# Scan of a state-space layer: u times D made by ScalarE in place and added as turns, in place of products with diagonals of D

## The reference, cut to what matters

```python
delta = softplus(dt_raw @ dt_proj_w.T + dt_proj_b)            # per token, 256 inner channels
A = -exp(A_log)
dA = exp(einsum('bti,is->btis', delta, A))                    # 16 states s
dBu = einsum('bti,bts->btis', delta * u, B_ssm)
h_t = dA_t * h_(t-1) + dBu_t                                  # the scan over 512 tokens
y_t = einsum('bis,bs->bi', h_t, C_t)
y = ys + u * D_param                                          # D_param: one number per inner channel
y = y * silu(z)
return y @ out_proj_w.T + residual
```

## Time and profile before

| | us |
|---|---|
| median of 3 runs | 1143.78 |
| the profiled execution's own time | 1146.79 |
| its span | 1144.8 |
| PE busy | 1031.4 (90%) |
| PEld busy | 797.5 (70%) |
| DVE busy | 896.6 (78%) |
| ACT busy | 822.5 (72%) |
| POOL busy | 516.9 (45%) |
| scans at L1084, x128 | 289.8 |
| idle of DVE before them | 31.7 |

### The profile page before, as it was taken

The page is one execution under the profiler, slowest core; times in us unless marked ns, Lnnn a source line. Parts: engine busy times, 40 slices in busy tenths (PEclk is TensorE's granted clock), DMA queues, the critical chain, the costliest instruction groups (busy, mean ns, idle before and its releaser), DMA issues. The chain is left out here.

```text
span 1144.8 us, 23452 instructions
## 1 busy us (share of the span) xinstructions
PE 1031.4 (90%) x7794; PEld 797.5 (70%) x7794; DVE 896.6 (78%) x1946; ACT 822.5 (72%) x1736; POOL 516.9 (45%) x322
## 2 busy tenths in 40 slices
PE   3876699999999999988997999999999999986997
PEld 3442589899899889858994555555555555555997
DVE  7698898889889888964764687878878787885565
ACT  4898898898988988735654676766767676761664
POOL 0288898898999988833550000110101010111354
PEclk9998699999999999999998999999999999998999
DMA  3000255555686676423332000000000000002331
GB/s 99 3 4 26 78 153 135 141 146 150 186 243 175 174 215 174 120 80 97 98 90 74 1 1 1 20 15 6 20 1 20 1 20 1 20 20 67 106 94 52
DMA packets 107782, 89.50 MB, mean 78 GB/s; under 512 B 35815, under 2 KB 85740, under 8 KB 107664
## 3 DMA queue, kind: packets, MB, share of 16 engines
q1 hardware_dynamic: 98784, 66.02, 22.1%
q0 software_dynamic: 5568, 12.66, 3.1%
q10 hardware_dynamic: 3312, 9.33, 2.7%
HBM read 71.49 MB, written 17.39 MB: 78 GB/s over the span
## 5 line engine op out<-in xcount | busy, mean ns | idle before, releaser
L1084 DVE TENSOR_TENSOR_SCAN h<-d_a,p_dbu 128x1024 f32<-128x1024 f32 x128 | 289.8, 2279 | 31.7 <-ACT d_a L828 26.5
L770 POOL TENSOR_TENSOR h<-h,c_rep 128x1024 f32<-128x1024 f32 x126 | 297.6, 2394 | 23.0 <-DVE h L1084 22.1
L1412 POOL DMA_INDIRECT expert_rows<-r_row,r_dest x60 | 59.6, 993 | 432.8 <-DVEq L1307 418.2
L828 ACT ACTIVATE d_a<-arena,a_exp 128x511 f32<-128x511 f32 x256 | 168.0, 710 | 13.5 <-DVE h L1084 13.4
L2152 DVE CUSTOM_DVE_ANT_0 arena<-at_p_scores,arena 128x512 f32<-128x512 f32 x256 | 162.4, 686 | 13.9 <-PE at_p_scores L1940 12.1
L2161 DVE COPY at_probs_T<-at_p_probs_T 128x512 f32<-128x512 f32 x128 | 88.0, 687 | 66.0 <-PE at_p_probs_T L1948 65.3
L2068 ACT ACTIVATE at_probs<-arena,at_min 128x512 f32<-128x512 f32 x145 | 98.3, 713 | 50.6 <-DVE at_min L2152 50.3
L976 PE MATMUL p_y_T<-ident,h 128*128 128x128 f32 x1024 | 133.4, 274 | 1.2 <-DVE h L1139 1.1
L820 ACT ACTIVATE b_du_T<-arena,b_T 128x256 f32<-128x256 f32 x304 | 128.7, 495 | 0.0
L1940 PE MATMUL at_p_scores<-arena,at_q_T 64*128 64x512 f32 x512 | 127.3, 615 | 0.0
L976 PEld LDWEIGHTS p_y_T<-ident,h 128*128 128x128 f32 x1024 | 116.7, 142 | 1.7 <-DVE h L1139 1.7
(11 more groups left out here) (285 smaller groups left out, 1763.3 us busy)
## 6 DMA issues: line engine op xcount, KB each, us to landing
c_rep<-c_rows SPq DMA_DIRECT2D x128, 256.0 KB
diag_b<-diag_rows SPq DMA_DIRECT2D x52, 256.0 KB, 4.2
f_row<-expert_rows SPq DMA_DIRECT2D x78, 129.0 KB
arena<-in_w_all ACTq DMA_DIRECT2D x8, 578.0 KB, 5.8
arena<-bias_by_distance ACTq DMA_DIRECT2D x8, 448.0 KB, 5.6
x_tok<-in_x SPq DMA_DIRECT2D x4, 512.0 KB, 5.9
x_tok<-x_between SPq DMA_DIRECT2D x8, 256.0 KB, 2.7
diag_rows<-diag_b SPq DMA_DIRECT2D x4, 256.0 KB
```

Of the source, the lines that this page charges most:

```text
L770: nc.gpsimd.tensor_tensor(h_at(n), h_at(n), cc, ALU.mult).then_inc(prod_done, 1)
L828: nc.scalar.activation(da[:, s % 2, ch, 1:], delta[:, one(b), ch, 1:].squeeze(1), ACT.Exp, scale=a_exp[:, ch, s:s + 1]).then_inc(da_ready, 1)
L1084: nc.vector.tensor_tensor_scan(h_at(n).rearrange("p c t -> p (c t)"), da[:, s % 2, :, :].rearrange("p c t -> p (c t)"), p_dbu[:, s % 2, :, ...
```

## The change

ScalarE multiplies u by D in place, one chunk of 128x512 at a time (`scale_u`): for batch 0 in its own states 1 and 2, behind the exponentials, and for every later batch in states 13 and 15 of the batch before, behind the exponentials. The multiplication is placed behind the last use of u itself: for batches 0 and 1 ScalarE waits until GpSimd has made du of that batch. `through_d` waits until both chunks of its batch are scaled, and then turns the tiles of the scaled u by the identity into `p_yT`, as `sum_up` does with h (`SUM_BY_TRANSPOSE` is True). The diagonals and the instructions that made them are gone; a tile of the same size keeps their place in memory, so nothing else moves.

```diff
--- before.py
+++ after.py
@@ -680,7 +680,7 @@
                     xlT=lambda b: zs[:, one(b), 0, :].squeeze(1), scratch=p_small[:, T // 2:])
         plan = Plan(k, "f1", c, h[:].rearrange("p n c t -> p (n c t)")[:, HS * NC * T - Plan.WORDS:])
         at.begin_flip(c, [p_dbu[:, 0, 0, :], p_dbu[:, 0, 1, :], p_dbu[:, 1, 0, :], p_dbu[:, 1, 1, :]])
-        diag_d = sb("diag_d", [P, NC, P])
+        sb("clear_of_x_dbc", [P, NC, P])
         da = sb("d_a", [P, 2, NC, T])
         rt.last_row = da[:].rearrange("p n c t -> p (n c t)")[:, 0:TPB * ROW].rearrange("p (j w) -> p j w", j=TPB)
         b_du = sb("b_du_T", [P, SR, TPB, DI])
@@ -689,7 +689,7 @@
         S = lambda n: k.sem("scan_" + n, c)
         a_ready, dve_step, act_step = S("a_ready"), S("dve_step"), S("act_step")
         c_in = [S(f"c_in{i}") for i in range(CR)]
-        diag_ready, zero_ready = S("diag_ready"), S("zero_ready")
+        u_scaled, zero_ready = S("u_scaled"), S("zero_ready")
         diag_zeroed, diag_filled = S("diag_zeroed"), S("diag_filled")
         diag_out, diag_in = [S(f"diag_out{i}") for i in range(DR)], [S(f"diag_in{i}") for i in range(DB)]
         du_turned, duT_ready = S("du_turned"), S("duT_ready")
@@ -828,10 +828,11 @@
                     nc.scalar.activation(da[:, s % 2, ch, 1:], delta[:, one(b), ch, 1:].squeeze(1), ACT.Exp,
                                          scale=a_exp[:, ch, s:s + 1]).then_inc(da_ready, 1)
 
-            def diagonals():
-                for ch in range(NC):
-                    ins = nc.scalar.activation(diag_d[:, ch, :], k.ident[:], ACT.Copy, scale=dpar[:, ch:ch + 1])
-                ins.then_inc(diag_ready, 1)
+            def scale_u(b, ch):
+                if b < 2:
+                    act.wait_ge(front.du_done, b + 1)
+                nc.scalar.activation(u[:, b, ch, :], u[:, b, ch, :], ACT.Copy,
+                                     scale=dpar[:, ch:ch + 1]).then_inc(u_scaled, 1)
 
             def take_g(b, ch):
                 act.wait_ge(g_turned, NC * b + ch + 1)
@@ -874,8 +875,10 @@
                     exps(b, s)
                     if number == 0 and s == 0:
                         front.last_log(act)
-                    elif number == 0 and s == 2:
-                        diagonals()
+                    elif number == 0 and s in (1, 2):
+                        scale_u(b, s - 1)
+                    if s in (13, 15) and not last:
+                        scale_u(b + 1, (s - 13) // 2)
                     if number > 0 and s == 11:
                         rt.act_normed(act, b - 1)
                     if load and s % 2:
@@ -957,12 +960,14 @@
                 mm.then_inc(dbu_ready, 1)
 
             def through_d(b):
+                pe.wait_ge(u_scaled, NC * b + NC)
                 if b > 0:
                     pe.wait_ge(gated, b)
                 for j in range(TPB):
                     for ch in range(NC):
                         nc.tensor.matmul(p_yT[:, j, ch * P:(ch + 1) * P],
-                                         u[:, one(b), ch, j * P:(j + 1) * P].squeeze(1), diag_d[:, ch, :],
+                                         u[:, one(b), ch, j * P:(j + 1) * P].squeeze(1), k.ident[:],
+                                         is_transpose=SUM_BY_TRANSPOSE,
                                          start=j % 2 == 0 and ch == 0, stop=False, skip_group_check=True)
 
             def sum_up(b, s):
@@ -1020,7 +1025,6 @@
                             pe.wait_ge(front.pos_ready, B * NC)
                             pe.wait_ge(front.abs_ready, B * NC)
                             pe.wait_ge(front.bT_ready, B)
-                            pe.wait_ge(diag_ready, 1)
                         through_d(b)
                     if s >= LAG:
                         sum_up(b, s - LAG)
```

## The result

The changed kernel takes 1149.17 us (median of 10 runs, 1144.79 to 1151.61) against 1144.32 of the kernel before on the same chip (1141.45 to 1147.87): ratio 1.0038, 95% interval 1.0020 to 1.0056. Later measurements on two other chips gave it 1.0033 (1.0015 to 1.0051) and, with three more filler products (products whose result nobody reads, which keep TensorE busy) ahead of the scans, 1.0035 (1.0019 to 1.0050). It is slower by about 4 us. One execution of the kernel before with those fillers took 2597.86 us, and no ratio here includes it. The forecast was no change, 1143.8, range up to 1147.5: wrong.

What follows compares the result with a forecast made beforehand. The prediction saw a chain changing hands within a batch, mostly successive scans, with ScalarE late in states 7 to 14. Gain 2.6 us and cost 2.6 us summed to 0.0: 1143.8 us, forecast's own range 1142.2 to 1145.4, overall 1140.0 to 1147.5.

Steps and rivals of the forecast that it cites:

- TensorE's work: State 4 of each batch: eight turns in 1.04 us replace products taking 2.05; 1.01 us less per batch, 8.1 in all.
- Behind it the sum of x, the next turn of du and the copies move with the scan, so the 0.35 us is kept: After the scan of state 7, batches 2 to 7: its 0.35 us gain lasts, 2.1 us; with batch 1's 0.5, 2.6.
- the second turn of g (0.14): Behind the spread of state 6, which needs the scan of state 4: only 0.14 of the 0.47 us gain passes.
- ScalarE's price: Activations in states 13 and 15 start the next batch's scan of state 0 0.43 us later; six transitions, 2.6 us.
- The clock: TensorE's clock at the start of the scans: expected at 1.00 from 138 again, with no cost in the sum.
- rival 4: Start of batch 0: turns alone don't raise TensorE's clock, which stays at 1.2 GHz to state 11; +6.3 us, 1150.1; 10%.
- Batch 0 to 1 "free": End of batch 0: VectorE's small copy ends at 170.30 whenever it starts, hiding a scan 0.3 us late; no cost.
- Sum: Whole execution: 2.6 us gained and 2.6 us lost give 0.0 us on the profiled 1146.79; median 1143.8.
- Rival 1: Scans of state 7 lose their whole wait, 4.7 us, and activations cost only 1.4; -3.8 us, 1140.0; 15%.
- Rival 2: TensorE is the bound throughout, so all its saved work counts: 8.1 us faster, 1135.7; 3%.
- Rival 3: ScalarE's queue has no slack in states 13 to 0, so both activations land in full; +5.3 us, 1149.1; 10%.

Runs made afterwards that it cites:

- kernel c: Changed kernel with u of the next batch scaled in states 2 and 5, not 13 and 15 (batch 0 as before): 1.0008 of the kernel before.

## Why the prediction was wrong

- **TensorE's work** (8 turns in 1.04, 1.01 less per batch): right (1.06). The scan of state 7 gains 0.33 to 0.34 for 0.35 forecast, in batch 1 0.5: right.
- **"Behind it the sum of x, the next turn of du and the copies move with the scan, so the 0.35 us is kept"**: this step failed. The turn of du does not move with the scan but with TensorE's queue, which is held by the scan of state 4 at the spread of state 6 and is busy without a gap from there to the turn of du (8.48 of 8.48 us). The prediction had this very limit for the second turn of g (0.14) and dropped it behind the scan of state 7. The queue kept 0.13 us, and the scan of state 10 came 0.12 earlier. On a quick chip batches 2 to 6 keep 0.12 to 0.14 each, batch 1 0.48, the last batch its 0.35: 0.48 + 5 x 0.13 + 0.35 = 1.5 instead of 2.6.
- **ScalarE's price** (6 x 0.43 = 2.6): right, by the place (state 0), the mechanism and nearly the size: +0.48 a batch with products, and 45.05 against 44.62 to 44.64 with turns, 0.42. So the batches that nothing disturbs sum to -1.5 + 2.5 = +1.0 us, not to 0.0.
- **The clock**, a term that the sum put at nothing. I looked at it only where it rises (rival 4, refuted). What it costs is mostly behind the wait ahead of state 12. A fall is about 1.6 us (47.10 against 45.51, 46.65 against 45.04 in the changed kernel with three more fillers); 11 in 60 batches against 1 in 36 is 0.9 more falls an execution, 1.5 us, an estimate that the executions' mean clock bears out. Filling the wait gave 1.6 to 2.2 us back (1.0033 to 1.0038 down to 1.0019).
- **Batch 0 to 1 "free"**: wrong in part of the executions. Two of the seven profiles with the copy and the scaling in state 13 of batch 0 lost 3.5 us there (2.3 by the copy, 1.2 by a fall of the clock behind it), 1.0 us on average; four without the scaling lost none. That few profiles make this a likely part, not a measured one.
- **Sum**: 1.0 + 1.5 + 1.0 = 3.5 us; the three ratios give 3.8 to 4.3. Only the 1.0 is read from rows throughout; the other two are averages over few profiles. The first pair of profiles suggested 2.5 us ahead of the scans; that was chance.
- Rival 1 (faster) falls: the scan of state 7 kept 0.29 of its wait, as forecast. Rival 2: 8.1 us less work on the engine with the fullest loads gained nothing by itself (1.0010 and 1.0004). Rival 3 was nearest in time (1149.1), but by luck: the slack that it denied was there, and both activations cost 0.42 to 0.48 a batch and not 1.22.

Open: whether and why the fillers cost the kernel before 1 to 2 us; how the copy can miss its turn; and, on the slower chips, why the scan of state 9 waits 0.4 to 2.0 us in many batches for nothing that the profile shows, so that batches are 45.1 to 45.6 there with and without the change.

## What to carry to other kernels

Follow a gain past the wait that it shortens, in the queue of every engine that hands something on. A queue that is busy without a gap passes on only what it gained at its last wait for something that didn't move. Taking work off an engine that already waits makes its waits longer, and for TensorE a longer wait can bring the clock down behind it, as in 10 of the 15 longest here: look at the longest waits in a period, not only at the start, and fill them. A tiny VectorE copy beside a GpSimd that never pauses can take a whole GpSimd instruction or two; read the duration against the work.

## What the runs showed of the hardware

- A copy of 128x8 on VectorE lasted 1.09, 2.03 to 2.39, or 4.35 to 4.36 us beside back-to-back GpSimd multiplies of about 2.4, each time to the end of one of them; a reduction of the same size 0.13 to 0.14.
- TensorE's clock fell from 2.4 to 1.2 GHz behind waits as short as 1.52 us in a stretch that was else busy, and stayed up behind one of 2.08.
- Turns alone raised the clock (at 141.0, after turns without a gap from 138.0) and held it (1.00 from 141.0 to 153.9, and for 15.9 us in the kernel before).
- The first scan's start agreed within 0.2 us in two pairs of profiles of one program (127.8 and 127.8; 125.3 and 125.1) and differed by 1.7 and 1.2 us in two others, the kernel before with the reduction (125.3 and 123.6) and kernel c with reduction and fillers (124.7 and 123.5). Agreement of one repeated profile doesn't make a difference the change's own.
